# Fused attention and feed-forward: the half-precision cast moves from VectorE to ScalarE, row sums from ones columns

## The reference

```
q, k, v = xn @ Wq + bq, xn @ Wk + bk, xn @ Wv + bv        # 16 heads of 32
scores  = q k^T / sqrt(32) + slope(h) * (key - 511), masked above the diagonal
ctx     = softmax(scores) @ v                             # per head
attn    = ctx @ Wo + bo
ffn     = (silu(xn @ gate^T) * (xn @ up^T)) @ down^T      # weights [2048, 512] from splines
out     = x + attn + ffn
```

## Time and profile before

| | us |
|---|---|
| median of 3 runs | 837.47 (837.46 to 837.83) |
| the profiled execution | 838.84 |
| its span, first to last instruction | 837.0 |
| TensorE busy | 711.5 (85%) |
| TensorE weight loads busy | 563.2 (67%) |
| VectorE busy | 507.2 (61%) |
| ScalarE busy | 439.3 (52%) |
| GpSimd busy | 332.3 (40%) |
| mean granted TensorE clock | 0.922 of full |

### The profile page before, as it was taken

One profiled execution on the slowest core, in us unless ns is written; L12 is line 12 of the kernel. 1 busy time (PEld: TensorE's weight loads), 2 busy tenths in 40 slices (PEclk: granted clock), 3 DMA queues, 4 the chain that ended last, 5 costly groups with the idle time before them and its releaser, 6 DMA issues. The chain is left out here.

```text
span 837.0 us, 14001 instructions
## 1 busy us (share of the span) xinstructions
PE 711.5 (85%) x4884; PEld 563.2 (67%) x4884; DVE 507.2 (61%) x1289; ACT 439.3 (52%) x961; POOL 332.3 (40%) x191
## 2 busy tenths in 40 slices
PE   5678779889789888898898676677978999999997
PEld 4556557667677776676676565455766888888886
DVE  6286687798979888967888688556432222222212
ACT  4266576687657766756877672334332333233321
POOL 2343453444534545534544450112214325425434
PEclk9878789899979999898999799679898999999999
DMA  7982654553584346465437945756616646433201
GB/s 254 188 219 37 111 74 155 76 76 65 114 182 101 48 76 114 93 173 77 67 68 210 252 143 170 245 153 187 208 51 196 224 118 202 153 108 105 101 1 50
DMA packets 53023, 109.78 MB, mean 131 GB/s; under 512 B 6361, under 2 KB 6617, under 8 KB 51417
## 3 DMA queue, kind: packets, MB, share of 16 engines
q1 hardware_dynamic: 51368, 106.46, 51.2%
q10 hardware_dynamic: 1584, 2.43, 1.2%
HBM read 59.32 MB, written 25.17 MB: 101 GB/s over the span
## 5 line engine op out<-in xcount | busy, mean ns | idle before, releaser
L1132 POOL TENSOR_TENSOR work<-work 128x1280 f16<-128x1280 f32 x64 | 168.4, 2632 | 235.2 <-DVE work L816 234.9
L1029 ACT ACTIVATE work<-work,neg_max 128x128 f32<-128x128 f32 (+3 forms) x256 | 142.3, 564 | 106.7 <-DVE neg_max L808 105.9
L1581 POOL TENSOR_TENSOR in_lo<-inner,in_hi 128x512 fp32r<-128x512 f32 x64 | 85.3, 1335 | 221.8 <-ACT in_hi L1497 221.8
L808 DVE CUSTOM_DVE_ANT_0 work<-bank,dist 128x128 f32<-128x128 f32 (+3 forms) x256 | 115.3, 487 | 89.0 <-PE bank L600 70.7
L1544 DVE TENSOR_TENSOR inner<-bank,silu 128x512 f32<-128x512 f32 x64 | 44.1, 689 | 136.0 <-ACT silu L1491 125.1
L1038 ACT COPY work<-bank 128x768 f16<-128x768 f16 (+1 forms) x128 | 110.0, 909 | 30.7 <-PE bank L614 29.5
L600 PE MATMUL bank<-k_stack,q_stack 96*128 96x256 f32 (+2 forms) x256 | 81.4, 396 | 45.2 <-issue 25.5
L1497 ACT CAST in_hi<-inner 128x512 fp32r<-128x512 f32 x64 | 39.7, 621 | 151.2 <-PE bank L1441 144.3
L614 PE MATMUL bank<-ident,work 128*128 128x128 f16 x1280 | 109.5, 230 | 10.2 <-DVE work L823 8.0
L614 PEld LDWEIGHTS bank<-ident,work 128*128 128x128 f16 x1280 | 78.4, 104 | 50.8 <-issue 35.2
L1439 PE MATMUL bank<-w_room,in_hi 128*128 128x512 f32 x256 | 102.7, 401 | 0.5 <-POOL in_lo L1581 0.5
(11 more groups left out here) (100 smaller groups left out, 1411.8 us busy)
## 6 DMA issues: line engine op xcount, KB each, us to landing
q_stack<-parts SPq DMA_DIRECT2D x48, 256.0 KB, 5.6
k_stack<-parts SPq DMA_DIRECT2D x48, 256.0 KB, 5.7
z<-xt_scratch SPq DMA_DIRECT2D x128, 88.0 KB
x_in<-x SPq DMA_DIRECT2D x32, 256.0 KB, 5.5
xt_scratch<-xt_room SPq DMA_DIRECT2D x8, 1024.0 KB, 6.8
xt_room<-xt_scratch SPq DMA_DIRECT2D x6, 1024.0 KB, 11.0
factor<-c_basis SPq DMA_DIRECT2D x5, 1024.0 KB, 7.9
taps<-windows SPq DMA_DIRECT2D x5, 1024.0 KB, 9.8
```

The costliest lines, as they stand in the source:

```text
L808: dve.tensor_tensor_reduce(probs[:, s % 2, OFF[i]:OFF[i] + n], score_bank[i % 2][:, 0:n], dist[:, S - n:S], -slope(s), 3.4e38, ALU.add, AL ...
L1029: e = act.activation(tile, tile, ACT.Exp, bias=neg_max[:, s % 2, i:i + 1], scale=-1.0, accum_out=row_sum[:, s % 4, i:i + 1])
L1132: pool.tensor_tensor(probs16[:, s % 2, 1, :], probs[:, s % 2, :], probs16[:, s % 2, 0, :], ALU.subtract).then_inc(lo_ready, 1)
L1581: pool.tensor_tensor(in_lo[k % 2][:, :], inner[:, k % 2, :], in_hi[:, k % 2, :].bitcast(F32), ALU.subtract).then_inc(il_ready, 1)
```

## The change

The cast of head s to fp16 moves from VectorE's step s+1 to ScalarE's step s, between the exponentials and the copies of turned tiles, with the same two waits. The exponentials no longer write row sums. Each head's values get two columns of 1.0 ahead of the three 32-column parts, so 98 and 66 columns are multiplied where 96 and 64 were; column 0 of each result is the row sum, which the reciprocal reads from PSUM. A memset writes the ones once. The value tile grows by 256 bytes per partition, and tiles placed after it, in the feed-forward part too, move up by that much.

```diff
-        v_parts = sb("v_parts", [P, QT, H, 3, HD], BF16)
+        v_parts = sb("v_parts", [P, QT, H, VALUES], BF16)      # VALUES = 2 + 3 * HD
...
-        row_sum = sb("row_sum", [P, 4, QT], F32)
...
-                    pe.matmul(bank[:, i * 96:(i + 1) * 96], probs_t[:, s % 2, at:at + P],
-                              v_parts[:, k, s, :, :], start=(k == 0), stop=False)
+                    pe.matmul(bank[:, i * VALUES:(i + 1) * VALUES], probs_t[:, s % 2, at:at + P],
+                              v_parts[:, k, s, :], start=(k == 0), stop=False)
...
-                    mm = pe.matmul(bank[:, i * 96:i * 96 + 64], probs_t[:, s % 2, at:at + P],
-                                   v_parts[:, k, s, 0:2, :], start=False, stop=(k == n - 1))
+                    mm = pe.matmul(bank[:, i * VALUES:i * VALUES + 2 + 2 * HD], probs_t[:, s % 2, at:at + P],
+                                   v_parts[:, k, s, 0:2 + 2 * HD], start=False, stop=(k == n - 1))
...
-            def probs_high(b, s):                              # VectorE
-                dve.wait_ge(p_ready, H * b + s + 1)
-                if later(b) or s >= 2:
-                    dve.wait_ge(pt_full, 4 * (H * b + s - 1))
-                dve.tensor_copy(probs16[:, s % 2, 0, :], probs[:, s % 2, :]).then_inc(hi_ready, 1)
...
-                dve.reciprocal(inv_sum[:, s % 2, :], row_sum[:, s % 4, :])
+                heads = av_bank[:, 0:QT * VALUES].rearrange("p (q n) -> p q n", q=QT)
+                dve.reciprocal(inv_sum[:, s % 2, :], heads[:, :, 0])
...
+            dve.memset(v_parts[:, :, :, 0:2].rearrange("p t h n -> p (t h) n"), 1.0).then_inc(small_set, 1)
...
             def exponentials(b, s):
-                if later(b) or s >= 4:
-                    act.wait_ge(av_read, H * b + s - 3)
...
                     e = act.activation(tile, tile, ACT.Exp, bias=neg_max[:, s % 2, i:i + 1],
-                                       scale=-1.0, accum_out=row_sum[:, s % 4, i:i + 1])
+                                       scale=-1.0)
                 e.then_inc(p_ready, 1)
+
+            def probs_high(b, s):                              # ScalarE
+                act.wait_ge(p_ready, H * b + s + 1)
+                if later(b) or s >= 2:
+                    act.wait_ge(pt_full, 4 * (H * b + s - 1))
+                act.copy(probs16[:, s % 2, 0, :], probs[:, s % 2, :]).then_inc(hi_ready, 1)
...
                 if s < H:
                     exponentials(b, s)
+                    probs_high(b, s)
                 if turned:
                     take_turned(*turned, 2)
```

More of the change, by code:

```diff
@@ L53 @@
 PROBS = 1280
+VALUES = 2 + 3 * HD
 def grid():
@@ L286, in build_kernel @@
         base = aligned(nc)
-        room = lambda name, shape, dt, at: nc.alloc_sbuf_tensor_at(name, shape, dt, offset=base + at * KB)
+        room = lambda name, shape, dt, at: nc.alloc_sbuf_tensor_at(name, shape, dt, offset=base + int(at * KB))
         wgu_hi = room("wgu_hi", [P, 2, NG, P], F32R, 0)
@@ L291, in build_kernel @@
         z = room("z", [P, NG, S], F32R, 42)
-        coef = room("coef", [P, 2, 512], F32R, 74)
-        in_lo = [room("in_lo0", [P, S], F32R, 78), room("in_lo1", [P, S], F32R, 40)]
+        coef = room("coef", [P, 2, 512], F32R, 74.25)
+        in_lo = [room("in_lo0", [P, S], F32R, 78.25), room("in_lo1", [P, S], F32R, 40)]
         def load_basis(sp):
@@ L792, in v_split @@
                 dve.wait_ge(vh_ready, n)
-                dve.tensor_tensor(full, full, v_parts[:, t, heads, 0, :], ALU.subtract).then_inc(v_rest, 1)
+                first, second, third = (v_parts[:, t, heads, 2 + part * HD:2 + (part + 1) * HD] for part in range(3))
+                dve.tensor_tensor(full, full, first, ALU.subtract).then_inc(v_rest, 1)
                 dve.wait_ge(v_rest, n)
-                dve.tensor_copy(v_parts[:, t, heads, 1, :], full).then_inc(v_mid, 1)
+                dve.tensor_copy(second, full).then_inc(v_mid, 1)
                 dve.wait_ge(v_mid, n)
-                dve.tensor_tensor(v_parts[:, t, heads, 2, :], full, v_parts[:, t, heads, 1, :],
-                                  ALU.subtract).then_inc(v_done, 1)
+                dve.tensor_tensor(third, full, second, ALU.subtract).then_inc(v_done, 1)
             def bias_and_max(b, s, tiles):
@@ L856, in step @@
             def step(b, s, carry, carried):
-                halved, turned, weighed = back(b, s, 1), back(b, s, 2), back(b, s, 3)
+                turned, weighed = back(b, s, 2), back(b, s, 3)
                 last = (s - 1) % H
@@ L1019, in v_high @@
                         act.wait_ge(av_full, H * (b - 1) + HALF * (half + 1))
-                act.copy(v_parts[:, t, heads, 0, :],
+                act.copy(v_parts[:, t, heads, 2:2 + HD],
                          v_full[:, t, :].rearrange("p (h d) -> p h d", h=H)[:, heads]).then_inc(vh_ready, 1)
             def exponentials(b, s):
-                if later(b) or s >= 4:
-                    act.wait_ge(av_read, H * b + s - 3)
                 for i in range(QT):
@@ L1087, in _ @@
             act.wait_ge(const_ld, 16 * 4)
-            act.wait_ge(small_set, 3)
+            act.wait_ge(small_set, 4)
             qk_high(0, "q", 0)
@@ L1339, in room @@
         def room(name, shape, dt, at):
-            return nc.alloc_sbuf_tensor_at(name, shape, dt, offset=base + at * KB)
-        bo_all = room("bo_all", [P, D], F32, 74)
-        bm = room("bm", [P, len(BM_PAIRS), 2, P], F32R, 80)
-        silu = room("silu", [P, 2, S], F32, 87)
-        inner = room("inner", [P, 2, S], F32, 91)
-        in_hi = room("in_hi", [P, 2, S], F32R, 95)
-        w_new = room("w_new", [P, 2, 512], F32, 99)
-        resid = room("resid", [P, QT, D], F32, 103)
-        mom_st = room("mom_st", [P, 2, 2, S], F32R, 111)
-        factor[3] = room("factor3", [P, 4, 512], F32, 103)
-        factor[4] = room("factor4", [P, 4, 512], F32, 103)
+            return nc.alloc_sbuf_tensor_at(name, shape, dt, offset=base + int(at * KB))
+        bo_all = room("bo_all", [P, D], F32, 74.25)
+        bm = room("bm", [P, len(BM_PAIRS), 2, P], F32R, 80.25)
+        silu = room("silu", [P, 2, S], F32, 87.25)
+        inner = room("inner", [P, 2, S], F32, 91.25)
+        in_hi = room("in_hi", [P, 2, S], F32R, 95.25)
+        w_new = room("w_new", [P, 2, 512], F32, 99.25)
+        resid = room("resid", [P, QT, D], F32, 103.25)
+        mom_st = room("mom_st", [P, 2, 2, S], F32R, 111.25)
+        factor[3] = room("factor3", [P, 4, 512], F32, 103.25)
+        factor[4] = room("factor4", [P, 4, 512], F32, 103.25)
         taps[3] = nc.alloc_sbuf_tensor_at("taps3", [P, 4, 512], F32, offset=w_at + 56 * KB)
```

8 lines of the change are left out of this document (3 added, 5 removed).

## The result

The changed kernel takes 824.37 us (median of 4 runs, 821.64 to 826.07) against 837.47: a ratio of 0.9841, 95% interval 0.9813 to 0.9868. That is 13.1 us faster. I had forecast 4.5 us, for 833.0. The profiled execution after took 826.07 us, its span is 824.3 against 837.0, and its mean granted clock 0.944 against 0.922.

A forecast was written before the change was run, and what follows sets the result against it. TensorE was taken as nearest to a bound, with stalls at group heads. Terms -2.1 +1.2 -3.1 +0.5 -1.0 gave -4.5 us: 834.3 against the profiled run, 833.0 against the median; likeliest case 829 to 836, with rivals 821 to 845.

The forecast's parts named there:

- Start-up: First batch, up to the group head at 67.72: K's remainder starts at 55.0 us instead of 58.12, -3.1 us.
- Rival B: Shorter stalls at group heads keep TensorE's clock up, 2.9 us at each of two heads: 827, at four 821; chance 0.22.
- Rival A: Evictions behind ScalarE's cast late in every Q/K step, 0.6 us each for TensorE: 846 or 844.7 us; chance 0.25.
- x turns: TensorE's transpositions of the next batch's x, steps 9 and 10: 0 gain, bounds 0 and 0.8 us at each of 6.
- The cast on ScalarE: Q/K step pairs: a 1.26 us cast delays evictions, TensorE loses 0.65 us per pair; where it counts, +1.2 us in all.
- The K path: K product, eviction, GpSimd's remainder, transfer: the remainder starts 0.25 to 0.5 us earlier, six boundaries at 0.35, -2.1 us.
- Columns: Value products: two more columns cost under 1 ns each over 1280 products, +0.5 us counted, bounds 0 and 5.
- The reciprocal: VectorE, each head: reading PSUM costs 0.05 us more, hidden in VectorE's idle time in dense steps.
- The end: End of the last batch: VectorE freed of the cast, ScalarE takes most of it away, -1.0 us, bounds -3 and +3.
- Rival C: No change: ScalarE later than assumed, K path +1 us instead of -2.1, 838.6 us, taken as 837; chance 0.13.

The follow-up runs named there:

- e2: The changed kernel with the cast left on VectorE in its old place, only the ones columns and no accumulator reads: 840.14 us, ratio 1.0018.
- e4: The changed kernel with ScalarE's cast behind its two copies of turned tiles instead of before them: 835.48 us, ratio 0.9974.
- e5: The kernel before with 24 extra unread products ahead of the first score product at nine group heads: 827.12 us, ratio 0.988.
- e9: The kernel before with 20 extra unread products ahead of the x turns of steps 9 and 10: 832.10 us, ratio 0.993.

## Why the prediction was right and wrong

The direction, the start-up and the two paths on ScalarE were right; one step failed, and it held more than all the others together. That 824.37 us lies inside the 821 to 845 that I gave for B and most of A, between B's own 827 and 821, is in part luck: it is below the 829 to 836 of the forecast, and more than half of the gain came at x turns that neither the forecast nor B has.

**The step that failed** is "the chain there runs through GpSimd: its remainder of head 8 starts at 225.51, behind the small power instruction", "With the cast gone VectorE reaches L839 some 0.3 us earlier and is held to the same 228.15. I cost the x turns at 0 gain". The chain is right, and L834 is still held by GpSimd after the change (220.88, 1.24 us). What was wrong is that I took its start as given. I named the power instruction but did not read its row: 1.32 us for two columns, in the same interval as the very cast that was to go. Its hold ran the other way from the one that I described, VectorE's instruction delaying GpSimd's. Steps 9 to 11 gave 7.4 us and the whole groups 10.0. My bound of 0.8 at each of 6 turns was too small, though for the hold alone it held (3.4 us, or 0.6 a turn); what exceeded it was the clock.

**Rival B, the clock,** was real, and I had asked only whether it or the forecast would come; both did. The heads at step 0 of batches 1 and 3 went from 8.50 and 8.54 us to 5.59, 2.9 each, exactly the term that B has, and the group of batch 1 gave back some of it (its step 3 went from 9.19 to 10.31). Over all nine heads the first steps took 64.5 us before and 57.7 after, with some heads slower (step 8 of batch 3 went from 5.57 to 7.16). B had been tied to the heads; at the x turns, where the clock gave 5.6 less 1.6 us, I had not looked, since I expected no stall there to change. In all, time below full clock fell from 130.7 to 93.1 us.

**Start-up** -3.1: the group gave -3.0. The remainder of head 1 starts at 54.26 and K's at 56.83, not 55.0 as I had it, because the whole start is 1.8 us later (the first score product at 39.73 instead of 37.97), for which I had nothing. In the profiles of the other kernels it comes at 38.3 to 39.6, in three without the added memset at 38.3 to 38.7; what moves it is open. So the head at step 4 comes only 1.3 us earlier, at 66.46 instead of 67.72.

```profile
52.92 1.26 ACT L1029 CAST work<-work 128x1280 f16<-128x1280 f32 x1
54.26 2.61 POOL L1131 TENSOR_TENSOR work<-work 128x1280 f16<-128x1280 f32 x1 [3.54 <-ACT work L1029]
56.83 1.46 POOL L1126 TENSOR_TENSOR parts<-qk_full,parts 128x512 fp32r<-128x512 f32 x1
```

**The cast on ScalarE**, 1.26 us and 0.65 a pair of lost time: 1259 ns, and the steps behind the pairs, 2, 6 and 14 of a batch, grew by 0.9, 0.4 and 0.7 us. The waits stand where I put them:

```profile
279.78 1.26 ACT L1029 CAST work<-work 128x1280 f16<-128x1280 f32 x1
280.94 1.71 ACT L1036 COPY work<-bank 128x768 f16<-128x768 f16 x2
...
281.88 0.27 PE L614 MATMUL bank<-ident,work 128*128 128x128 f16 x2 [0.51 <-ACT work L1036]
```

Rival A needed them in every Q/K step. There were 33, in steps 2, 3, 6, 7, 14 and 15 and at the end. Where they count, it is as much as I had put down: steps 2 and 3 together took 15.36 us in batch 1 before and 15.81 in batch 2 after, both at full clock, 0.45 more against my 0.4.

**The K path** -2.1, 0.35 a boundary: its start in the step came 0.3 us earlier in pair (0,1) (11.06 to 10.75) and 0.6 in pair (4,5) (11.33 to 10.75), where I had 0.25 and 0.5. With six boundaries that is right. But the stalls are nine, not the eight that I counted, so there were seven such boundaries; and the stretches between them are not free of gaps over 0.4 us, as I had it: step 3 of batch 1 has two of 1.3 us. **Columns** +0.5: successive products and their means (214 and 198 ns against 215 and 200) did not change, nor did e2's groups; about 0. **The reciprocal** from PSUM costs 8 ns more, not 50. **The end** -1.0: +2.6 for batch 3 from step 8 on, within the bounds of -3 to +3 and of the wrong sign; TensorE's waits for ScalarE there are up to 2.0 us long, and its first step alone lost 1.6 us to the clock.

Rival C had the K path turned by a late ScalarE. That is what e4 makes of it, at 835.5 us; in the changed kernel it did not occur. In the chances, the 0.62 for faster is the forecast and B alone, with nothing of C in it.

## What to carry to other kernels

Before an engine's operation is costed as hidden, find every instruction of the engine that shares its memory port in the same interval, and compare its length with the same form elsewhere: a small instruction that is twice as long as it can be is the first link of a chain. A stall that shrinks can be worth more than its own length, by what the clock gives back, so price stalls in TensorE's stream with the row of the same steps at both levels, at every stall that changes and not only at the largest. And when a producer becomes earlier, ask whom its consumer will now hold.

## What the hardware showed that I had not expected

- GpSimd's power of 128x2 elements takes 0.69 us and 1.32 beside VectorE's 1280-column cast from fp32 to fp16; means 721 and 1194 ns over 8.
- Two normalising instructions of 512 columns on VectorE took 0.99 us in the open, 1.94 beside one GpSimd subtraction, and 4.24 when two GpSimd subtractions followed each other.
- 216 unread products in the waits for K stacks made the kernel 10.7 us faster (e5, against 837.8 beside it), and 120 ahead of the x turns 5.7 (e9); in the latter the clock over steps 9 to 11 went from 0.82 to 0.88 up to 1.00.
- The cast from fp32 to fp16 in SBUF took 827 ns on VectorE and 1259 on ScalarE, and the kernel was faster with the slower one. The Trainium skill, "ScalarE: Activation LUTs", section "Rules for kernel authors", would leave plain arithmetic on VectorE for its speed per element. The two durations agree with it, and the 13.1 us do not: what decided was which engine the cast held up.
